# Opening of an attention stage on one Trainium2 core: constant rows by DMA, first columns loaded ahead on two queues, third heads' loads moved

## The chip, the cores and the metric

The program runs on one core of a Trainium2 chip, as one launch. The metric is the device time of one execution in microseconds (us). Beside each time stands a profile of one execution, taken by the hardware profiler.

## The reference, cut to what matters

The input x is 4 sequences of 2048 positions by 256 channels. The program computes one attention block and one mixture-of-experts block, each with a layer norm ahead and a residual around it:

```python
q_lat, k_lat, v_lat = x @ Wq_down, x @ Wk_down, x @ Wv_down   # 16 heads x 64
q = concat([q_lat @ Wq_up_c, rope(q_lat @ Wq_up_e)])          # 16 numbers a head
k = concat([k_lat @ Wk_up_c, rope(k_lat @ Wk_up_e)])
scores = (q @ k.T) / sqrt(16)                                 # causal, 2048 x 2048
y = softmax(scores) @ (v_lat @ Wv_up)
x = x + y @ Wc                                                # attention
x = x + sum over the top 2 of 8 experts (relu MLP, 256-512-256)
```

The change touches only the attention between the projections and y.

## The kernel before, in words

The program has several stages, one block each, with a barrier between them. `project` computes q, k and v for all heads and writes them to HBM (`parts_dram`, `v_dram`). `attend` reads them back and writes y. `mix` and the expert stage follow. In the profiled execution `project` ends and `attend` begins at about 284.8 us.

Fp32 accuracy comes from splitting q and k each into a high and a low part (`fp32r`). A head's stack in SBUF, in `q_st` and `k_st`, has three groups of 16 rows (`DH` = 16, `STACK` = 48): high, high, low of q against high, low, high of k. Two heads lie side by side in the partitions, one in partitions 0 to 63 and one in 64 to 127 (`par` 0 and 1, `HALF_ROWS` = 64). Rows 48 and 49 of each half are two more rows (`PARTS` = 2): in `q_st` they hold minus the row maximum of the scores, in two parts, and in `k_st` the constant 1.0, so that one matmul over 50 rows (`ROWS`) gives the score minus its maximum. The matmuls that only look for the maximum use the 48 rows.

The 16 heads of 4 sequences are worked through in 16 groups of four heads of one sequence (`NG` = 16, number w; three buffers, `BUFS` = 3, so group w uses buffer w % 3). One group is loaded by 13 DMAs on SP's queue (`load`, L717 to L731): 12 of 256 KB, each 16 rows by 2 head pairs by 2048 columns into 16 partitions of `q_st` or `k_st`, so packets of 8 KB; and one of 544 KB into `v_sb`, all 128 partitions. In the order of issue `q_st` and `k_st` alternate, so each set of 16 partitions is written by two DMAs in a row. All 13 increment the semaphore `loaded[u]`.

For each group the kernel does two passes. The maximum pass ("max" pieces): for a tile of 128 queries (`qt`, 16 of them), a pair of heads and a block of 512 keys (`kc`), two matmuls at L939 write a PSUM bank of `ps_m`, and VectorE (DVE) takes its maximum at L831 (whole blocks) or L835 (blocks on the diagonal, with the causal mask added). The tiles are taken in two turns: early (`qt` 0 to 11, `EARLY` = 12) and late (12 to 15). A turn ends with "chain" (L850, the negated maximum), "turn_max" (a transpose on TensorE at L946, the two parts at L860 and L862) and `place_minus` on SP: `minus_rows` goes to `minus_dram` (L736), SP waits for it, and two DMAs bring it into `q_st` rows 48 and 49 (L742). Only then may the scores pass of those queries start: matmuls at L904, exponentials on ScalarE (ACT) at L810 or L806, the diagonal mask on GpSimd (POOL) at L788, sums over the keys at L922 ("sum"), then "turn_out" (L950, L869, L874) and the store of y (L757).

All engines follow one list, `PLAN`, written by `attention_plan` from modelled costs. The change leaves it as it is. `SLOTS` = 2 banks of `ps_m` let TensorE be two pieces ahead of DVE.

The opening of the stage, which the change touches:

- POOL makes the identity, clears `maxes`, makes `causal`, then fills rows 32 to 63 of `k_st` with 1.0 for all three buffers (L778).
- DVE clears `ps_o` (L820), then fills rows 96 to 127 of `k_st` with 1.0 (L822). Each fill increments `ones_made`.
- SP waits for `ones_made` = 2 (L745), then issues the loads of groups 0, 1 and 2, 39 DMAs in a row, and goes on to the plan.
- TensorE (PE) waits for the identity, for `ones_made` = 2 and for `ps_o` to be clear. At the first max piece of a group it waits for all 13 DMAs of the load (`loaded[w % 3]` = 13 * 16).
- ACT has no work before the first scores.

The queues: SP's DMAs go to one hardware queue (q1 in the profile) over the core's 16 DMA engines. ACT's DMAs go to another. Both use the same 16 engines.

Of the kernel before, what the change touches and what calls it, by code (L numbers as in the profile page):

```python
# [15 lines left out]
TB = 512  # L16
# [622 lines left out]
def attend(nc, parts_dram, v_dram, minus_dram, y_dram):  # L639
# [17 lines left out]
    with ExitStack() as ctx:  # L657
        def sb(name, shape, dt):
            return ctx.enter_context(nc.sbuf_tensor(name, shape, dt))

        def sem(name):
            return ctx.enter_context(nc.semaphore(name))
# [10 lines left out]
        junk = sb("junk", [P, SLOTS, 2, TB], F32)  # L673
        maxes = sb("maxes", [P, GH, QT, CH], F32)
        minus = sb("minus", [P, GH * EARLY], F32)
        minus_rows = sb("minus_rows", [GH * EARLY, PARTS, P], F32R)

        ps_s = [ctx.enter_context(nc.psum_tensor(f"ps_s{i}", [P, 2 - i, 512], F32)) for i in range(2)]
# [3 lines left out]
        ident_made = sem("ident_made2")  # L682
        causal_made = sem("causal_made")
        ones_made = sem("ones_made")
        maxes_clear = sem("maxes_clear")
        banks_clear = sem("banks_clear")
        loaded = [sem(f"loaded{u}") for u in range(BUFS)]
# [26 lines left out]
        def turn_number(w, late):  # L714
            return 2 * w + (1 if late else 0)

        @block.sync  # L717
        def _(sp):
            def load(g):
                b, hg, u = g // HG, g % HG, g % BUFS  # L720

                for i, (of_q, of_k) in enumerate(((0, 0), (0, 1), (1, 0))):
                    for par in range(2):
                        rows = slice(par * HALF_ROWS + i * DH, par * HALF_ROWS + (i + 1) * DH)
                        for to, t, of in ((q_st, 0, of_q), (k_st, 1, of_k)):
                            sp.dma_start(to[rows, u, :, :].bitcast(F32),
                                         parts_v[t, of, :, :, hg:hg + 1, :, par, b * T:(b + 1) * T].rearrange(
                                             "f j g pr n -> (f j) (g pr) n")).then_inc(loaded[u], 16)
                sp.dma_start(v_sb[:, u, :, :, :].rearrange("p k h d -> p (k h d)"),
                             v_dram[hg, :, b * QT:(b + 1) * QT, :, :].rearrange("p k h d -> p (k h d)")  # L730
                             ).then_inc(loaded[u], 16)  # L731

            def place_minus(w, late):
                lo, n = (EARLY, QT - EARLY) if late else (0, EARLY)

                sp.dma_start(minus_dram[late][:, :, :, :].rearrange("s h k n -> (h k) s n"),  # L736
                             minus_rows[0:GH * n, :, :].bitcast(F32)).then_inc(rows_out, 16)
                sp.wait_ge(rows_out, 16 * (turn_number(w, late) + 1))
                from_v = minus_dram[late].rearrange("s (pr par) k n -> s pr par (k n)", par=2)
                for par in range(2):  # L740
                    rows = slice(par * HALF_ROWS + STACK, par * HALF_ROWS + ROWS)
                    sp.dma_start(q_st[rows, w % BUFS, :, lo * P:(lo + n) * P].bitcast(F32),  # L742
                                 from_v[:, :, par, :]).then_inc(rows_in, 16)

            sp.wait_ge(ones_made, 2)  # L745
            for g in range(BUFS):
                load(g)
            for e, ring in plan_with_ring():
                if e[0] == "turn_max":
                    sp.wait_ge(piece_taken, ring + 1)  # L750
                    place_minus(e[1], e[2])
                elif e[0] == "turn_out":
                    w, c = e[1] // CH, e[1] % CH
                    sp.wait_ge(piece_taken, ring + 1)
                    to = y_dram[(w // HG) * T + c * TB:(w // HG) * T + (c + 1) * TB,
                                (w % HG) * (GH * DH):(w % HG + 1) * (GH * DH)]
                    sp.dma_start(to.rearrange("(j p) n -> p j n", p=P),  # L757
                                 y_sb[:, c % 2, :, :, :].rearrange("p j h d -> p j (h d)")
                                 ).then_inc(y_stored[c % 2], 16)
                elif e[0] == "sum" and (e[1] + 1) % NSTEP == 0 and (e[1] + 1) // NSTEP + BUFS - 1 < NG:  # L760

                    sp.wait_ge(summed, e[1] + 1)
                    load((e[1] + 1) // NSTEP + BUFS - 1)
            for i in range(2):
                sp.wait_ge(y_stored[i], 16 * (NG * CH // 2))

        @block.gpsimd
        def _(pool):
            make_identity(nc, pool, ident, ident_made)
            nc.gpsimd.memset(maxes[:, :, :, :], NEG).then_inc(maxes_clear, 1)  # L770

            nc.gpsimd.memset(causal[:, :], 0.0).then_inc(causal_made, 1)
            pool.wait_ge(causal_made, 1)
            nc.gpsimd.affine_select(out=causal[:, TB - P:TB], in_=causal[:, TB - P:TB], compare_op=ALU.is_ge,
                                    fill=NEG, base=0, pattern=[[-1, P]],
                                    channel_multiplier=1).then_inc(causal_made, 1)
            pool.wait_ge(causal_made, 2)
            nc.gpsimd.memset(k_st[32:64, :, :, :].bitcast(F32), 1.0).then_inc(ones_made, 1)  # L778
            for s, (_, c, kt) in enumerate(STEP_LIST):
                r = kt - c * TILES  # L780
                if r < 0:
                    continue
                for pair in range(2):

                    pool.wait_ge(exp_made, COVERS[s][2 * pair + 1] + 1)
                    at = (s % PROBS) * GH + 2 * pair
                    tile = prob[:, at:at + 2, r * P:(r + 1) * P]
                    nc.gpsimd.affine_select(out=tile, in_=tile, compare_op=ALU.is_ge, fill=0.0, base=0,  # L788
                                            pattern=[[0, 2], [1, P]], channel_multiplier=-1).then_inc(masked, 1)

        @block.scalar
        def _(act):
            for e in PLAN:
                if e[0] == "scores":
                    k = e[1]
                    bank = ps_s[k % 2]
                    newest = GROUPS[k][-1][0]
                    if newest >= PROBS:

                        act.wait_ge(summed, newest - PROBS + 1)  # L800
                    act.wait_ge(scores_made, k + 1)
                    at = (GROUPS[k][0][0] % PROBS) * GH + GROUPS[k][0][1]
                    lows = [STEP_LOW[s] for s, _ in GROUPS[k]]
                    if len(lows) == 2 and lows[0] != lows[1]:
                        for i, lo in enumerate(lows):
                            last_exp = nc.scalar.activation(prob[:, at + i, lo:TB], bank[:, i, lo:TB], ACT.Exp,  # L806
                                                            scale=DH ** -0.5)
                    else:
                        n, lo = len(lows), lows[0]
                        last_exp = nc.scalar.activation(prob[:, at:at + n, lo:TB], bank[:, 0:n, lo:TB], ACT.Exp,  # L810
                                                        scale=DH ** -0.5)
                    last_exp.then_inc(exp_made, 1)
                elif e[0] == "sum" and STEP_LAST[e[1]]:

                    act.wait_ge(summed, e[1] + 1)
                    nc.scalar.copy(out_sb[:, STEP_LIST[e[1]][1], :], ps_o[:, :]).then_inc(out_copied, 1)

        @block.vector
        def _(dve):
            nc.vector.memset(ps_o[:, :], 0.0).then_inc(banks_clear, 1)  # L820

            nc.vector.memset(k_st[96:128, :, :, :].bitcast(F32), 1.0).then_inc(ones_made, 1)  # L822
            dve.wait_ge(causal_made, 2)
            dve.wait_ge(maxes_clear, 1)

# [52 lines left out]
        @block.tensor  # L878
        def _(pe):
            pe.wait_ge(ident_made, 2)  # L880
            pe.wait_ge(ones_made, 2)
            pe.wait_ge(banks_clear, 1)

            def half(par, rows):
                return slice(par * HALF_ROWS, par * HALF_ROWS + rows)

            loads_seen = rows_seen = 0
            for e, ring in plan_with_ring():
                slot = ring % SLOTS
                if e[0] == "scores":  # L890
                    k = e[1]
                    w, c, _ = STEP_LIST[GROUPS[k][-1][0]]
                    placed = turn_number(w, c == CH - 1) + 1
                    if placed > rows_seen:

# [13 lines left out]
                elif e[0] == "sum":  # L909
                    s = e[1]  # L910
                    w, c, kt = STEP_LIST[s]
                    r = kt - c * TILES
                    lo = STEP_LOW[s]
                    if STEP_FIRST[s] and s:

                        pe.wait_ge(out_copied, CH * w + c)
# [9 lines left out]
                else:  # L926
# [3 lines left out]
                        pe.wait_ge(piece_taken, ring - SLOTS + 1)  # L930
                    if e[0] == "max":
                        _, w, qt, pair, kc = e
                        if w + 1 > loads_seen:

                            pe.wait_ge(loaded[w % BUFS], LOADS * 16 * (w // BUFS + 1))
                            loads_seen = w + 1
# [988 lines left out]
```

## Time and profile before

| | us |
|---|---|
| three timed runs | 2747.91, 2764.52 (median), 2771.68 |
| the profiled execution | 2749.61 |
| its span, first to last instruction | 2747.7 |
| start of `attend` in it | 284.8 |
| first load DMA issued | 298.43 |
| first max matmul | 329.43 |
| first scores matmul | 391.41 |
| PE, DVE, ACT, POOL busy (us of the span) | 2398.2, 2107.0, 1569.7, 772.5 |

The profiled execution took 1.9 us more than its span. Times in the rows below are microseconds from the start of the span. PE is TensorE's matmul, PEld its weight load, DVE is VectorE, ACT is ScalarE, POOL is GpSimd. SPq, ACTq and POOLq are the DMA-issuing instructions of those engines.

### The profile page before, as it was taken

To read this page: it belongs to the slowest core of one execution; us is meant where nothing else is said; L and a number is where in the kernel's file an instruction comes from. 1 tells how busy PE (TensorE), PEld (TensorE's weight loads), DVE (VectorE), ACT (ScalarE), POOL (GpSimd) and SP (SyncE) were. 2 spreads that over 40 slices of the span, in tenths; PEclk is the share of its full clock that TensorE was granted. 3 is DMA by queue.
4 is the path that set the end of the run, shared out by engine and by line. 5 is a ranking of instruction groups with operands and counts; after the bars stand their busy time and mean duration, and the time that the engine had idled before them with its cause. 6 is when DMAs were issued, how large, how long until landed. Compare 5 with 4: busy or idle time off the path is not lost. (4 is left out here: it accounts for less than half of the span.)

```text
span 2747.7 us, 49305 instructions
## 1 busy us (share of the span) xinstructions
PE 2398.2 (87%) x15842; PEld 1364.3 (50%) x15842; DVE 2107.0 (77%) x5154; ACT 1569.7 (57%) x2668; POOL 772.5 (28%) x1051
## 2 busy tenths in 40 slices
PE   6777179999999999999999999999879669999997
PEld 6666033333333333333333333333246458889896
DVE  3998398999899888887888998896038657777775
ACT  2444016777677677676667777777745424444442
POOL 1555200110110110110110110110107646766553
PEclk7888559999899999998899999999989879999999
DMA  4999760431430440440431440400059633333332
GB/s 149 338 335 319 126 83 5 63 46 23 61 50 19 61 60 9 61 59 10 61 40 29 63 51 17 64 7 6 9 226 263 170 114 105 105 118 107 113 110 64
DMA packets 154501, 255.60 MB, mean 93 GB/s; under 512 B 72563, under 2 KB 95605, under 8 KB 145568
## 3 DMA queue, kind: packets, MB, share of 16 engines
q1 hardware_dynamic: 129760, 191.47, 32.3%
q0 software_dynamic: 22736, 55.48, 6.1%
q10 hardware_dynamic: 1776, 5.72, 0.5%
q8 instruction: 129, 2.11, 0.4%
q14 instruction: 100, 0.82, 0.1%
HBM read 147.59 MB, written 107.76 MB: 93 GB/s over the span
## 5 line engine op out<-in xcount | busy, mean ns | idle before, releaser
L810 ACT ACTIVATE prob<-ps_s 128x512 f32<-128x512 f32 (+5 forms) x1620 | 1078.4, 714 | 522.2 <-PE ps_s L904 519.3
L831 DVE TENSOR_REDUCE maxes<-ps_m 128x2 f32<-128x1024 f32 x768 | 913.7, 1221 | 117.1 <-PE ps_m L939 114.2
L939 PE MATMUL ps_m<-k_st,q_st 48*128 48x512 f32 (+3 forms) x2560 | 611.8, 447 | 115.4 <-DMA v_sb<-v_dram 58.4
L904 PE MATMUL ps_s<-q_st,k_st 50*128 50x512 f32 (+3 forms) x2560 | 612.4, 414 | 74.6 <-ACT prob L810 56.8
L788 POOL TENSOR_SCALAR_AFFINE_SELECT prob<-prob 128x256 f32<-128x256 f32 x512 | 203.2, 406 | 1485.9 <-ACT prob L810 1355.2
L922 PE MATMUL ps_o<-prob,v_sb 128*17 128x512 f32 (+3 forms) x5120 | 618.6, 557 | 1.2 <-ACT prob L810 0.7
L939 PEld LDWEIGHTS ps_m<-k_st,q_st 48*128 48x128 f32 x2560 | 278.1, 194 | 577.3 <-DVE maxes L831 257.1
L835 DVE CUSTOM_DVE_ANT_0 junk<-ps_m,causal 128x128 f32<-128x128 f32 (+3 forms) x1024 | 453.2, 484 | 76.0 <-PE ps_m L939 74.0
L904 PEld LDWEIGHTS ps_s<-q_st,k_st 50*128 50x128 f32 x2560 | 320.5, 191 | 300.7 <-ACT prob L810 228.8
L1703 ACT ACTIVATE h_hi<-ps_turned 128x512 fp32r<-128x512 f32 x142 | 85.0, 598 | 214.2 <-PE ps_turned L1820 214.2
L922 PEld LDWEIGHTS ps_o<-prob,v_sb 128*17 128x17 f32 x5120 | 86.9, 96 | 171.6 <-issue 143.0
L91 PE MATMUL ps_out<-experts_hi,h_lo 128*128 (+1 forms) x568 | 171.7, 302 | 0.0
L93 PE MATMUL ps_out<-experts_hi,h_hi 128*128 (+1 forms) x568 | 160.4, 282 | 0.0
L92 PE MATMUL ps_out<-experts_lo,h_hi 128*128 (+1 forms) x568 | 160.0, 282 | 0.0
L1735 DVE TENSOR_TENSOR h<-ps_hidden,b_sb 128x512 f32<-128x512 f32 x142 | 98.2, 691 | 45.5 <-PE ps_hidden L93 44.7
L1749 DVE TENSOR_TENSOR y<-ps_out,b_sb 128x256 f32<-128x256 f32 x142 | 60.3, 424 | 87.7 <-PE ps_out L93 87.2
L91 PE MATMUL ps_hidden<-experts_hi,x_lo 128*128 (+1 forms) x284 | 126.0, 444 | 0.7 <-issue 0.5
L1124 POOL DMA_INDIRECT list_dram<-entry,slots x100 | 96.8, 968 | 79.2 <-DVE slots L1388 52.1
L93 PE MATMUL ps_hidden<-experts_hi,x_hi 128*128 (+1 forms) x284 | 113.0, 398 | 0.0
L92 PE MATMUL ps_hidden<-experts_lo,x_hi 128*128 (+1 forms) x284 | 112.9, 398 | 0.0
L92 PEld LDWEIGHTS ps_out<-experts_lo,h_hi 128*128 128x128 f32 x568 | 107.6, 189 | 0.1
L869 DVE RECIPROCAL rec<-ps_m 128x16 f32<-128x16 f32 x64 | 16.2, 253 | 118.9 <-PE ps_m L950 118.0
(183 smaller groups left out, 3181.4 us busy)
## 6 DMA issues: line engine op xcount, KB each, us to landing
parts_dram<-parts SPq DMA_DIRECT2D x64, 512.0 KB, 3.6
q_st<-parts_dram SPq DMA_DIRECT2D x96, 256.0 KB, 15.4
k_st<-parts_dram SPq DMA_DIRECT2D x96, 256.0 KB, 17.1
v_dram<-v_out SPq DMA_DIRECT2D x16, 544.0 KB, 4.7
v_sb<-v_dram SPq DMA_DIRECT2D x16, 544.0 KB, 25.4
xin<-in_L_attn_x SPq DMA_DIRECT2D x16, 512.0 KB, 4.7
ffn_raw<-in_L_ffn_W SPq DMA_DIRECT2D x32, 256.0 KB, 4.9
split_hi<-ffn_hi SPq DMA_DIRECT2D x16, 512.0 KB, 4.9
```

The source lines that it names most:

```text
L91: nc.tensor.matmul(out, s_lo, m_hi, start=first, stop=False, skip_group_check=True)
L92: nc.tensor.matmul(out, s_hi, m_lo, start=False, stop=False, skip_group_check=True)
L93: return nc.tensor.matmul(out, s_hi, m_hi, start=False, stop=last, skip_group_check=True)
L788: nc.gpsimd.affine_select(out=tile, in_=tile, compare_op=ALU.is_ge, fill=0.0, base=0, pattern=[[0, 2], [1, P]], channel_multiplier=-1).the ...
L810: last_exp = nc.scalar.activation(prob[:, at:at + n, lo:TB], bank[:, 0:n, lo:TB], ACT.Exp, scale=DH ** -0.5)
L831: return nc.vector.tensor_reduce(maxes[:, 2 * pair:2 * pair + 2, qt, kc], bank[:, :, :], AX.X, ALU.max)
L835: last = nc.vector.tensor_tensor_reduce(junk[:, slot, i, 0:w], bank[:, i, 0:w], causal[:, TB - w:TB], 1.0, NEG, ALU.add, ALU.max, maxes[:, ...
L904: mm = nc.tensor.matmul(ps_s[k % 2][:, i, lo:TB], k_st[half(h % 2, ROWS), w % BUFS, h // 2, kt * P:(kt + 1) * P], q_st[half(h % 2, ROWS), ...
L922: mm = nc.tensor.matmul(ps_o[32 * h:32 * h + VW, lo:TB], v_sb[:, w % BUFS, kt, h, :], prob[:, (s % PROBS) * GH + h, lo:TB], start=STEP_FIR ...
L939: mm = nc.tensor.matmul(ps_m[slot][:, i, 0:wide], q_st[half(i, STACK), w % BUFS, pair, qt * P:(qt + 1) * P], k_st[half(i, STACK), w % BUFS ...
L1124: pool.indirect_dma_start(list_dram[:, :], bass.IndirectOffsetOnAxis(ap=slots[:, j, i:i + 1], axis=0), entry[:, j, i, :], None).then_inc(s ...
L1735: nc.vector.tensor_tensor(out=h[:, s % 2, :], in0=ps_h[s % 2][:, :], in1=b1_sb[:, bass.ds(e, 1), :].rearrange("p a n -> p (a n)"), op=ALU. ...
```

## The change

What it does:

- A new tile `ones` (2 partitions by 2048) is filled with 1.0 by DVE, in place of the two fills of 32 partitions by 12288. ACT brings it into rows 48, 49 and 112, 113 of `k_st` by two DMAs of 96 KB each, all three buffers at once (`ones_placed`).
- The loads of group 0 are cut by columns. Columns 0 to 511 come first: six DMAs of 64 KB for `q_st` on SP's queue and six for `k_st` on ACT's queue, all on `first_loaded`. The remaining 1536 columns (twelve DMAs of 192 KB) and v (544 KB) follow on SP's queue.
- Group 1 is loaded by ACT's queue, after the constant rows. Group 2 is loaded by SP's queue, issued after the `place_minus` of the first turn. In all loads the six DMAs of `q_st` now come before the six of `k_st`, and consecutive DMAs write different sets of 16 partitions.
- SP waits for nothing at its start. PE waits for `first_loaded` before the plan, for `loaded[0]` at the first max piece with `qt` of 4 or more, and for `ones_placed` before the first scores. The wait for `loaded` is also looked at by the "sum" entries.

```diff
+        ones = sb("ones", [PARTS, T], F32)
...
+        def load_heads(eng, g, t, lo, hi, done):
+            b, hg, u = g // HG, g % HG, g % BUFS
+            to, pieces = ((q_st, (0, 0, 1)), (k_st, (0, 1, 0)))[t]
+
+            for i, of in enumerate(pieces):
+                for par in range(2):
+                    rows = slice(par * HALF_ROWS + i * DH, par * HALF_ROWS + (i + 1) * DH)
+                    eng.dma_start(to[rows, u, :, lo:hi].bitcast(F32),
+                                  parts_v[t, of, :, :, hg:hg + 1, :, par, b * T + lo:b * T + hi].rearrange(
+                                      "f j g pr n -> (f j) (g pr) n")).then_inc(done, 16)
+
+        def load(eng, g):
+            b, hg, u = g // HG, g % HG, g % BUFS
+            for t in range(2):
+                load_heads(eng, g, t, TB if g == 0 else 0, T, loaded[u])
+            eng.dma_start(v_sb[:, u, :, :, :].rearrange("p k h d -> p (k h d)"),
+                          v_dram[hg, :, b * QT:(b + 1) * QT, :, :].rearrange("p k h d -> p (k h d)")
+                          ).then_inc(loaded[u], 16)
+
         @block.sync
...
-            sp.wait_ge(ones_made, 2)
-            for g in range(BUFS):
-                load(g)
+            load_heads(sp, 0, 0, 0, TB, first_loaded)
+            load(sp, 0)
             for e, ring in plan_with_ring():
                 if e[0] == "turn_max":
                     sp.wait_ge(piece_taken, ring + 1)
                     place_minus(e[1], e[2])
+                    if turn_number(e[1], e[2]) == 0:
+                        for g in range(2, BUFS):
+                            load(sp, g)
...
-            nc.gpsimd.memset(k_st[32:64, :, :, :].bitcast(F32), 1.0).then_inc(ones_made, 1)
...
         @block.scalar
         def _(act):
+            load_heads(act, 0, 1, 0, TB, first_loaded)
+            act.wait_ge(ones_made, 1)
+            for par in range(2):
+                rows = slice(par * HALF_ROWS + STACK, par * HALF_ROWS + ROWS)
+                act.dma_start(k_st[rows, :, :, :].bitcast(F32).rearrange("p u a n -> p (u a) n"),
+                              ones[:, :].unsqueeze(1).broadcast_to([PARTS, BUFS * 2, T])).then_inc(ones_placed, 16)
+            load(act, 1)
...
-            nc.vector.memset(k_st[96:128, :, :, :].bitcast(F32), 1.0).then_inc(ones_made, 1)
+            nc.vector.memset(ones[:, :], 1.0).then_inc(ones_made, 1)
...
-            pe.wait_ge(ones_made, 2)
             pe.wait_ge(banks_clear, 1)
...
+            pe.wait_ge(first_loaded, LOADS // 2 * 2 * 16)
             for e, ring in plan_with_ring():
...
+                    if k == 0:
+                        pe.wait_ge(ones_placed, 2 * 16)
...
+                    if w + 1 > loads_seen:
+                        pe.wait_ge(loaded[w % BUFS], LOADS * 16 * (w // BUFS + 1))
+                        loads_seen = w + 1
...
-                        if w + 1 > loads_seen:
+                        if w + 1 > loads_seen and (w or qt >= TILES):
```

## Rows read from the trace of the kernel before

**Rows 1.** The page, parts 1 and 2: busy time, and the DMA engines' share in 40 slices.
```profile
PE 2398.2 (87%) x15842; PEld 1364.3 (50%) x15842; DVE 2107.0 (77%) x5154; ACT 1569.7 (57%) x2668; POOL 772.5 (28%) x1051
...
DMA  4999760431430440440431440400059633333332
```

**Rows 2.** Waits of all engines, 284 to 330: engine line waited for, total, times, longest.
```profile
PE ps_m L939 <- DMA v_sb<-v_dram: 58.4, 1, 58.4
```

**Rows 3.** Waits of SP's own queue, 280 to 384.
```profile
SPq L726 <- DVE k_st L822: 13.7, 1, 13.7
```

**Rows 4.** Timeline, 276 to 394: start, duration, engine line operation.
```profile
284.81 0.20 POOL L98 MEMSET ident<- 128x128 f32 x1 [6.78 <-POOLq L121]
...
288.10 10.30 DVE L822 MEMSET k_st<- 32x12288 f32 x1 [2.62 <-issue]
298.43 0.37 SPq L726 DMA_DIRECT2D q_st<-parts_dram  x1
298.84 0.42 SPq L726 DMA_DIRECT2D k_st<-parts_dram  x1
299.31 0.42 SPq L726 DMA_DIRECT2D q_st<-parts_dram  x1
...
303.50 0.42 SPq L726 DMA_DIRECT2D k_st<-parts_dram  x1
303.96 0.42 SPq L729 DMA_DIRECT2D v_sb<-v_dram  x1
...
311.90 1.07 SPq L726 DMA_DIRECT2D k_st<-parts_dram  x1
```

**Rows 5.** DMA issues of four short windows from 298.2 on: us from issue to landing.
```profile
q_st<-parts_dram SPq DMA_DIRECT2D x1, 256.0 KB, 4.6
k_st<-parts_dram SPq DMA_DIRECT2D x1, 256.0 KB, 6.3
q_st<-parts_dram SPq DMA_DIRECT2D x1, 256.0 KB, 8.2
...
v_sb<-v_dram SPq DMA_DIRECT2D x1, 544.0 KB, 25.3
k_st<-parts_dram SPq DMA_DIRECT2D x1, 256.0 KB, 23.9
```

**Rows 6.** Windows: PE, PEld, DVE, ACT, POOL busy, granted clock, DMA share, GB/s.
```profile
6.00:9.00 3.00, 0.00 (x0) 0.00 (x0) 0.00 (x0) 0.00 (x0) 0.00 (x0) 1.00 1.04 430
...
300.30:327.40 27.10, 0.00 (x0) 0.00 (x0) 0.00 (x0) 0.00 (x0) 0.00 (x0) 0.50 1.02 123
```

**Rows 7.** DMA issues of 0 to 20: SP's queue beside POOL's.
```profile
down<-in_L_attn_Wk_down SPq DMA_DIRECT2D x1, 1024.0 KB, 8.9
down<-in_L_attn_Wv_down SPq DMA_DIRECT2D x1, 1024.0 KB, 13.9
...
cos<-in_rope_cos POOLq DMA_DIRECT2D x1, 1024.0 KB, 9.1
```

**Rows 8.** Timeline of DVE, 329 to 425.
```profile
330.09 0.29 DVE L835 CUSTOM_DVE_ANT_0 junk<-ps_m,causal 128x128 f32<-128x128 f32 x1 [31.69 <-PE ps_m L939]
...
337.23 1.22 DVE L831 TENSOR_REDUCE maxes<-ps_m 128x2 f32<-128x1024 f32 x1
...
381.22 0.35 DVE L850 TENSOR_REDUCE minus<-maxes 128x48 f32<-128x192 f32 x1
...
421.10 0.28 DVE L835 CUSTOM_DVE_ANT_0 junk<-ps_m,causal 128x128 f32<-128x128 f32 x1
```

**Rows 9.** Timeline, 384 to 407: SP's queue and the first scores.
```profile
384.37 0.31 SPq L736 DMA_DIRECT2D minus_dram<-minus_rows  x1
385.97 1.51 SPq L742 DMA_DIRECT2D q_st<-minus_dram  x2
391.41 1.05 PE L904 MATMUL ps_s<-q_st,k_st 50*128 50x512 f32 x3
406.11 0.40 SPq L757 DMA_DIRECT2D y_dram<-y_sb  x1
```

More of the change, by code:

```diff
@@ L684, in attend @@
         ones_made = sem("ones_made")
+        ones_placed = sem("ones_placed")
+        first_loaded = sem("first_loaded")
         maxes_clear = sem("maxes_clear")
@@ L715, in turn_number @@
             return 2 * w + (1 if late else 0)
+        def load_heads(eng, g, t, lo, hi, done):
[14 more added lines that the diff above has]
+                          ).then_inc(loaded[u], 16)
         @block.sync
         def _(sp):
[L719 to L731, printed above, removed]
             def place_minus(w, late):
@@ L762, in _ @@
                     sp.wait_ge(summed, e[1] + 1)
-                    load((e[1] + 1) // NSTEP + BUFS - 1)
+                    load(sp, (e[1] + 1) // NSTEP + BUFS - 1)
             for i in range(2):
```

## The prediction

> **What bounds the kernel now.** I read the page first: PE is the busiest engine over the whole span, 87%, DVE is at 77%, and the DMA engines are full only in the first slices, around one tenth of the span and at the start of the last stage [rows 1]. A share over the span says nothing of the opening of one stage, so next come the waits in the stretch where `attend` begins. One wait is far longer than all others: PE sits idle 58.4 us before its first max matmul, until the load of v of group 0 has landed [rows 2]. The stage itself begins at 284.8, when POOL comes through the barrier [rows 4]. The queue's own waits say why the load came so late: SP waited 13.7 us for DVE's fill of `k_st`, which runs from 288.1 to 298.4 [rows 3, 4]. So the opening has three parts: 13.7 us of fill, from 284.8 to 298.4; 31 us of load, from 298.4 to 329.4; and then the maximum pass of the first turn, which DVE bounds: its pieces follow each other from 330.1 to the chain at 381.2 [rows 8]. The scores start at 391.4 after the trip of the maxima through HBM [rows 9]. Nothing of the later work can start before that, so what the opening gains or loses goes into the time in full.
>
> **The load in numbers.** The first 256 KB were issued at 298.43 and landed 4.6 us later, at 303.0; the twelfth was issued at 303.50 and landed 23.9 later, at 327.4; v landed at 303.96 + 25.3 = 329.3 [rows 4, 5]. Eleven DMAs in 24.4 us are 2.22 us for each 256 KB, 118 GB/s, and v took 1.9 us. The first one's 4.6 us less 2.2 leave 2.4 us from issue until data flow. In this stretch the 16 DMA engines show as fully busy (1.02) at 123 GB/s, while in the first microseconds of the program they moved 430 at the same share [rows 6]. The engines are thus full with transfers that write 16 partitions each, and slow ones.
>
> **Change, part 1: the start without the fill.** The fills of 10.3 us on POOL and DVE go. SP and ACT issue their first DMAs at about 284.8. Data flow from 287.2. The first columns are 12 x 64 KB = 768 KB, three units of 256 KB: 3 x 2.22 = 6.7 us, so 293.9. DVE's first piece follows 0.8 us after landing, as at 329.3 to 330.1 [rows 5, 8], at 294.7. The eight pieces of the first four tiles took from 330.09 to 337.23, 7.1 us [rows 8], so they end at 301.8, where DVE was at 337.2 before. If the rest of group 0 were there, 35.4 us would be gained. It is not: what is late next is the load of the other 1536 columns.
>
> **Part 2: the rest of group 0 beside group 1.** This decides. SP's queue holds 12 x 192 KB = 2304 KB and v; ACT's queue holds 12 x 256 KB = 3072 KB and v. ACT can issue them from about 290 on: DVE's fill starts at 288.1 and a fill of 2048 columns in place of 12288 takes a sixth of 10.3, 1.7 us. So both queues flow from about 294, with as many packets (6 KB against 8 KB). How do two queues share the engines? In the first stage SP's queue and POOL's ran side by side. Wv_down, issued one step of 0.5 us behind Wk_down, took 13.9 us to land against 8.9: 5.5 us for its 1.05 MB, while `cos` was on its way by POOL's queue [rows 7] and the engines moved 430 GB/s, 2.4 MB in 5.5 us [rows 6]. SP's queue had a little under half, and the engines' share stood at 1.04 [rows 6]. With equal shares of packets, the rest of group 0 ends only when group 1 is nearly in: 5376 KB, 21 units of 256 KB, 21 x 2.22 = 46.6 us, and 2 x 1.9 = 3.8 for both v. That is 344.3, and DVE takes its first whole block 1.0 us later, at 345.3. Before it was at 337.2: **8.1 us later than before**, at the old rate. In general, with r the rate of both queues together over the old 118 GB/s, DVE resumes at 293.9 + 3.8 + 1.0 + 46.6 / r and the change is 46.6 / r - 38.5 us. It is nothing at r = 1.21.
>
> **What r is.** The trace of before has no two queues with 16-partition writes, so it is bounded. Low: the k_st DMA that follows a q_st DMA on the same partitions lands 2.1 us after it (303.0 to 305.1), the one that turns to new partitions 2.4 us later (305.1 to 307.5) [rows 4, 5]. Now every DMA turns to new ones; at 2.4 us each, r = 2.22 / 2.4 = 0.925, and the change is +11.9 us. High: v, over all 128 partitions, went at 544 KB in 1.9 us, 2.5 times the rate [rows 5], so the engines can do more when more partitions are written at once. If the queues did not disturb each other at all, SP's needs 9 x 2.22 = 20.0 us and v 1.9: group 0 is in at 315.8, DVE resumes at 316.8, 20.4 us earlier. I take r = 1.1, nearest to the row in which two queues gave no more than one, with a little for engines that write different partitions at one moment: 42.4 - 38.5 = **+3.9 us**.
>
> The Trainium skill has a rule that speaks against this change. "SBUF — State Buffer", section "Can I just issue two DMAs to hit both halves?", says that two concurrent DMAs to partitions 0 and 64 gave only 6% more than one, since both run on the same 16 engines. By that, r is 1.06 and the sum 44.0 - 38.5 = +5.5 us, an estimate from that page. No row here shows it for these writes.
>
> **Part 3: constant rows.** Two DMAs of 96 KB into two partitions. The nearest row is the pair that brings the maxima into two partitions: 2 x 24 KB, issued from 385.97, and the scores start at 391.4, so at most 5.4 us for 48 KB [rows 9]. Four times the bytes are at most 22 us; at the rate of the 16-partition DMAs they would be 1.7 us. Issued at 290 they are in by 312, and needed at about 391. Cost nothing, with 80 us of cover. What they do to the queue behind them is a rival below.
>
> **Part 4: order, ACT's issues, group 2.** ACT issues 6 + 2 + 13 DMAs of some 0.47 us [rows 4], 10 us in all, while it has no other work until 391. SP's issues began to take longer (1.07) only at the 29th in a row [rows 4]; ACT has 21 and SP 19. Group 1 is in by 344 to 366 and wanted at 421.1 [rows 8]. Group 2's 13 DMAs are issued after SP's row DMAs at about 387.5, for 6.1 us, and SP's next work is the store at 406.1 [rows 9]. Its bytes then flow for some 28 us beside the scores, where before they were over at 385.6. Behind them in the queue stands the store of y, which may land some 10 us late; nothing waits for it until that buffer is used again two stores on. At nothing, up to 1 us if a row DMA meets them. The extra waits on PE are met when it comes there. From DVE's resumption on, the 43.9 us to the chain at 381.2 and all after it stay as they are.
>
> **Sum.** Start earlier, load shared: +3.9 us. The profiled execution, 2749.6, would be 2753.5. It is at the lower end of what was shown; the median of the runs is 14.9 above it. The mean of all four executions is 2758.4, and with +3.9 that gives 2762, which I forecast. It lies between the sums made on the profiled execution and on the median (2768).
>
> **Rivals.** (a) The queues add up, or nearly: r of 1.5 to 2 or more, -7.4 to -20.4 us. For it: v's rate, and that each set of 16 partitions is a bottleneck of its own. Against: rows 7, and engines that are busy at 1.02 with one queue. 2738 in full. (b) Slower: the turn to new partitions costs at each DMA, in the load of group 0; r under 1, price +11.9 us at 0.925; it decides from r below 1.21 on. For it: 2.4 against 2.1. Against: those two may be one lag seen twice. 2770. (c) Group 1 trails. If the two constant DMAs hold ACT's queue for 10 us, SP's queue moves 4.5 units alone; 10.5 are left, 23.3 / 1.1 = 21.2 us; group 0 is in at 293.9 + 10 + 21.2 + 3.8 = 328.9, DVE resumes at 329.9: -7.3 us, 2751. For it: writes into two partitions are slow. Against: nothing shows that they hold all 16 engines. That the start does not come forward at all is excluded by the wait for the fill, which is the only one between the barrier and the first load.
>
> **How the numbers follow.** Forecast (r 1.0 to 1.3, -3 to +8 us) 0.45, (a) 0.25, (b) 0.15, (c) 0.15. The forecast's own range is 2756 to 2767. The range runs from (a), 2758.4 - 20.4 = 2738, to (b) on the mean of the four, 2770, and 6 more because a median of a few runs may lie that far above the mean, as it does here: 2776. One per cent is 27 us, about what a measurement of this kernel can tell from no change; even (a) is only 20 us. Faster by over 1%: 0.04; within 1%: 0.93; slower: 0.03.
>
> **What would show it.** SP's first issue at 285. A first DVE piece at 293 to 296; if later, part 1 is wrong. Then a second wait of PE on a DMA, from about 302 to X, where X is group 0's landing: 340 by the forecast, 316 by (a), 348 by (b), 329 by (c). GB/s between 294 and 340: near 130 by the forecast, above 200 by (a). The first scores at 391.4 + 3.9 = 395.3. Wrong would be a wait anywhere after the scores start that grew by more than 2 us.

## The result, and the profile after

The changed kernel takes 2741.52 us (median of 20 runs, 2715.57 to 2771.07), the kernel before 2757.69 (20 runs, 2734.73 to 2782.83): ratio 0.9927, 95% interval 0.9901 to 0.9953. The ratio leaves out runs more than 1.5% above the fastest of their kernel (slow ones), so it gives 20 us, where the medians of all runs differ by 16. I forecast 2762 and a change of +3.9 us. The number lies in my range, the direction is wrong.

The profiled execution took 2743.78 us, its span 2741.9. The opening does almost what the prediction said. First the waits of all engines in 276 to 400:

```profile
PE ps_m L960 <- DMA v_sb<-v_dram: 39.5, 1, 39.5
PE ps_m L960 <- DMA k_st<-parts_dram: 22.3, 1, 22.3
```

Where before one wait of 58.4 us stood [rows 2], there are two, 62 us together. The timeline of the same stretch:

```profile
285.64 2.79 ACTq L727 DMA_DIRECT2D k_st<-parts_dram  x6
285.65 0.20 POOL L98 MEMSET ident<- 128x128 f32 x1 [6.78 <-POOLq L121]
...
288.52 1.96 ACTq L806 DMA_DIRECT2D k_st<-ones  x2
...
294.21 0.69 PE L960 MATMUL ps_m<-k_st,q_st 48*128 48x128 f32 x4 [22.32 <-DMA k_st<-parts_dram]
...
339.97 0.90 PE L960 MATMUL ps_m<-k_st,q_st 48*128 48x512 f32 x4 [39.50 <-DMA v_sb<-v_dram]
...
395.00 1.05 PE L922 MATMUL ps_s<-q_st,k_st 50*128 50x512 f32 x3
```

The first columns are in at 294.1 (forecast 293.9, for a stage that starts 0.8 us earlier), the rest of group 0 at 339.9 (forecast 340), the first scores start at 395.0 (forecast 395.3; before 391.4 [rows 9]). So the opening is 3.6 us later on the clock of the span, 2.7 us longer from the stage's start. It is not where the gain is. The window of 300 to 340:

```profile
300.00:340.00 40.00, 0.50 (x4) 0.06 (x2) 2.09 (x8) 0.00 (x0) 0.00 (x0) 0.50 0.96 140
```

Two queues move 140 GB/s, against 123 with one [rows 6]. Both windows hold some of v's bytes, which flow faster. In windows that end before v begins to flow (at 324.8), before and after, it is 117 against 136:

```profile
301.00:324.00 23.00, 0.00 (x0) 0.00 (x0) 0.00 (x0) 0.00 (x0) 0.00 (x0) 0.50 1.02 117
```

```profile
296.00:324.00 28.00, 3.41 (x12) 1.30 (x10) 5.94 (x24) 0.00 (x0) 0.00 (x0) 0.50 1.02 136
```

The gain lies behind the opening. `minus_dram<-minus_rows` (L736, now L744) happens twice for each group of heads, so it marks the time like a clock. Lines of it from SP's timeline, of before:

```profile
483.05 0.32 SPq L736 DMA_DIRECT2D minus_dram<-minus_rows  x1
...
578.04 0.32 SPq L736 DMA_DIRECT2D minus_dram<-minus_rows  x1
...
1906.62 0.33 SPq L736 DMA_DIRECT2D minus_dram<-minus_rows  x1
```

and of after:

```profile
387.95 0.31 SPq L744 DMA_DIRECT2D minus_dram<-minus_rows  x1
...
486.75 0.32 SPq L744 DMA_DIRECT2D minus_dram<-minus_rows  x1
...
581.64 0.32 SPq L744 DMA_DIRECT2D minus_dram<-minus_rows  x1
...
1893.78 0.33 SPq L744 DMA_DIRECT2D minus_dram<-minus_rows  x1
```

From the first to the last it is 384.37 to 1906.62 = 1522.3 us before [rows 9] and 1505.8 after: 16.5 us less in a part of the program in which the change leaves the work of PE, DVE, ACT and POOL alone; only the order of DMAs within a load and the place of group 2's load differ. From there to the end of the span the profiled execution of the changed kernel is 7.0 us longer (848.1 against 841.1), so the two profiled executions differ by 5.8 us in all, and their mean granted clocks are 0.924 before and 0.923 after: one pair of traces does not show the whole gain. In an undisturbed group there is no difference (578.04 - 483.05 = 95.0 us before; 581.64 - 486.75 = 94.9 after). The differences, of both signs, are in the groups in which the granted clock falls in one kernel and not in the other; most of the 16.5 us comes between 1111 and 1480. One such place is the load of a group near 1206. SP's timeline of before:

```profile
1212.14 0.42 SPq L729 DMA_DIRECT2D v_sb<-v_dram  x1
1212.61 0.43 SPq L736 DMA_DIRECT2D minus_dram<-minus_rows  x1
1236.94 1.23 SPq L742 DMA_DIRECT2D q_st<-minus_dram  x2
1238.21 2.95 SPq L757 DMA_DIRECT2D y_dram<-y_sb  x3
```

A turn's rows are written right behind the thirteen DMAs of a load, in the same queue. They land when the load has landed, 24 us later. SP waits for them, and three stores of y stand behind that wait. Then the windows of before, with PE, PEld, DVE, ACT, POOL busy, granted clock, DMA share and GB/s:

```profile
1236.00:1240.00 4.00, 3.46 (x28) 1.63 (x24) 2.93 (x7) 2.80 (x7) 1.22 (x3) 1.00 0.22 50
1240.00:1244.00 4.00, 3.17 (x20) 1.47 (x20) 3.20 (x7) 1.40 (x5) 1.17 (x3) 0.70 0.23 53
1244.00:1248.00 4.00, 4.00 (x26) 1.80 (x26) 1.98 (x5) 1.83 (x4) 0.77 (x2) 0.50 0.00 0
1248.00:1252.00 4.00, 3.46 (x18) 1.91 (x18) 3.03 (x7) 2.97 (x4) 0.00 (x0) 0.50 0.00 0
1252.00:1256.00 4.00, 4.00 (x21) 0.97 (x13) 2.31 (x6) 1.35 (x3) 0.00 (x0) 0.59 0.01 4
```

and of after:

```profile
1236.00:1240.00 4.00, 3.92 (x32) 1.63 (x24) 3.38 (x8) 2.80 (x6) 1.22 (x3) 1.00 0.22 52
1240.00:1244.00 4.00, 3.19 (x32) 1.73 (x33) 3.50 (x10) 2.17 (x7) 1.82 (x5) 1.00 0.24 55
1244.00:1248.00 4.00, 3.42 (x27) 1.57 (x23) 3.73 (x11) 3.51 (x5) 0.11 (x1) 1.00 0.00 0
1248.00:1252.00 4.00, 4.00 (x30) 1.42 (x28) 3.55 (x7) 2.79 (x5) 0.00 (x0) 1.00 0.01 4
```

PE's first matmul behind the wait, before and after:

```profile
1240.83 0.50 PE L939 MATMUL ps_m<-k_st,q_st 48*128 48x512 f32 x2 [1.37 <-DVE y_sb L874]
```

```profile
1240.81 0.50 PE L960 MATMUL ps_m<-k_st,q_st 48*128 48x512 f32 x2 [0.89 <-DVE y_sb L890]
```

Before, PE idled for 1.4 us until DVE had written `y_sb`, which waited 1.1 us for a store of y; then the clock was granted at 0.50, the lower of its two levels (1.2 GHz), for some 14 us. In 1244 to 1248 PE looks full (4.00), while DVE is busy for 1.98 us where it is 3.73 after. After, the same wait is there, but shorter (0.6 us of DVE, 0.9 of PE), and no fall follows. Over 395 to 1960 the waits of DVE for a store of y, before and after:

```profile
DVE y_sb L874 <- DMA y_dram<-y_sb: 4.9, 5, 1.6
```

```profile
DVE y_sb L890 <- DMA y_dram<-y_sb: 0.8, 2, 0.6
```

So the theory that the experiments had to test was: the new order of the DMAs in a load makes each later load some 2 to 3 us shorter (31.0 us before and 28.6 after, from first issue to landing, as the mean of the thirteen later loads), fewer stores of y come too late, and the granted clock falls less often.

### The profile page after: what moved, and what is told of

Read it like the earlier page. It is cut to its first block and busy times, and to the rows that moved or that the text cites. A ratio compares the mean times of both kernels' runs of the same rounds, so it can differ in the third digit from the quotient of the medians.

```text
span 2741.9 us, 49320 instructions
## 1 busy us (share of the span) xinstructions
PE 2395.7 (87%) x15842; PEld 1360.0 (50%) x15842; DVE 2098.7 (77%) x5154; ACT 1570.1 (57%) x2668; POOL 762.0 (28%) x1050
```

## The experiments

All were timed beside the kernel before. They ran on three chips, on which the kernel before itself takes 2871 to 2882 us (medians of 27 to 29 runs), so only their ratios are compared with the result and with each other.

**The changed kernel again.** 

> The changed kernel once more. Its first profile shows the first scores at 395.0 (before: 391.4), so an opening that is 3 us longer, but the timed runs are 0.73% (20 us) faster. Theory A (the profiled execution is not typical, the landing of group 0 varies from execution to execution): here the landing is 15 us or more away from 339.9. Theory B (the new order of DMAs in the loads of all later groups helps) and theory C (the granted clock in the rest of the attention is higher): landing within 3 us of 339.9 again, ratio near 0.993. If the 0.73% was chance, ratio within 0.3% of 1.

Ratio 0.9928 (0.9892 to 0.9963). PE resumed at 341.4 and the scores began at 396.4, 112.1 us after the stage start (109.4 in the first profile, 106.6 before). The gain is real and the late landing is typical: theory A falls. In this profile DVE waited 1.6 us for a store at 1239, and the lower clock followed for 14 us: the changed kernel is not free of these falls.

**The order alone.** The kernel before with

```diff
-                for i, (of_q, of_k) in enumerate(((0, 0), (0, 1), (1, 0))):
-                    for par in range(2):
-                        rows = ...
-                        for to, t, of in ((q_st, 0, of_q), (k_st, 1, of_k)):
+                for to, t, ofs in ((q_st, 0, (0, 0, 1)), (k_st, 1, (0, 1, 0))):
+                    for i, of in enumerate(ofs):
+                        for par in range(2):
+                            rows = ...
```

> The kernel before with the new order of DMAs in every load and nothing else. Theory B: ratio 0.992 to 0.995, with fewer or shorter falls of the granted clock after the first scores. Theories A and C: within 0.3% of 1; the opening then shows what the order alone does to the rate: first max matmul at 329.4 if the order is worth nothing, 2 to 3 us later if each turn to new partitions costs 2.4 us in place of 2.2, earlier by 2 us or more if alternating partitions is a gain.

Ratio 0.9941 (0.9902 to 0.998): nearly the whole gain of the change, with nothing of its new opening. The wait for group 0 and a window in the load:

```profile
PE ps_m L939 <- DMA v_sb<-v_dram: 55.6, 1, 55.6
```

```profile
298.00:321.00 23.00, 0.00 (x0) 0.00 (x0) 0.00 (x0) 0.00 (x0) 0.00 (x0) 0.50 1.02 135
```

PE waits 2.8 us less than the 58.4 of before [rows 2], and the load runs at 135 GB/s where the like window of before has 117, on one queue. The expected sign of fewer or shorter falls is not in this kernel's one profile, which is among its slower runs: the mean granted clock over 395 to 1960 is 0.96, as before. Over all its runs the mean clock is higher (0.9148 against 0.9101).

**Only the fill taken away.** Constant rows by two small DMAs on ACT's queue, SP's 39 loads at once, in the old order.

```diff
-            sp.wait_ge(ones_made, 2)
...
+            act.wait_ge(ones_made, 1)
+            for par in range(2):
+                rows = slice(par * HALF_ROWS + STACK, par * HALF_ROWS + ROWS)
+                act.dma_start(k_st[rows, :, :, :]..., ones[:, :]...).then_inc(ones_placed, 16)
```

> The kernel before with constant rows by two small DMAs on ACT's queue; SP starts its 39 loads at once in the old order, on one queue, nothing cut by columns. All theories agree on the opening: first max matmul at 329.4 - 13.7 = 315.7, first scores at 377.7. If the opening passes into the time in full the ratio is 0.995 (-13.7 us). Less than half of that would say that the opening's gain is given back later, by the granted clock or by waits.

Ratio 0.9992 (0.9955 to 1.003), and the opening did not move. SP's first issue and PE's first matmul:

```profile
285.17 0.37 SPq L728 DMA_DIRECT2D q_st<-parts_dram  x1
```

```profile
330.98 0.69 PE L945 MATMUL ps_m<-k_st,q_st 48*128 48x128 f32 x4 [59.57 <-DMA v_sb<-v_dram]
```

Group 0 took 45.8 us in place of 31. The 208 increments of its semaphore show why: 199 are there at 316.0, 15 us before the last, and the last eight come in four pairs from 318.7 to 330.8, as if two of the sixteen engines were far behind the others. All theories had missed this. In the changed kernel only the last pair lags, by 4 us (335.7 to 339.8).

**The constant rows issued after group 0.** The same, with ACT waiting for group 0 first:

```diff
             act.wait_ge(ones_made, 1)
+            act.wait_ge(loaded[0], LOADS * 16)
```

> The fill-only experiment with the two constant DMAs issued after group 0 has landed. There two of the 16 engines' shares of group 0 landed 15 us late. If the constant rows cost this, group 0 lands 31 us after the stage start (at 316), the opening is 13.7 us shorter than before and the ratio is 0.995. If they did not, it lands at 331 again and the ratio is near 1.

```profile
315.34 0.69 PE L946 MATMUL ps_m<-k_st,q_st 48*128 48x128 f32 x4 [45.06 <-DMA v_sb<-v_dram]
...
381.63 1.19 PE L911 MATMUL ps_s<-q_st,k_st 50*128 50x512 f32 x3 [4.11 <-DMA q_st<-minus_dram]
```

Group 0 is in 31.3 us after the stage start at 284.0, so the two small DMAs had cost 14.5 us of transfer time. The first scores then wait 4.1 us for their rows, which stand behind the load of group 2 in SP's queue, so the opening is 9.0 us shorter than before (97.6 against 106.6), not 13.7. The ratio is 0.9891 (0.9853 to 0.993), but its ten runs have a median of 2883, no lower than that of the kernel before (2882), and spread from 2841 to 2898, so whether the shorter opening shows in the time stays open.

**Group 1 waits for group 0.** The changed kernel with

```diff
+            act.wait_ge(loaded[0], LOADS * 16)
             load(act, 1)
```

> The changed kernel, but ACT waits until group 0 has landed before it loads group 1. If the two queues share one rate, as I forecast, group 0 lands at 294 + 20.0 + 1.9 = 316 in place of 340, and the first scores come at 371, 24 us earlier than in the changed kernel. Theory A or C with an opening that passes in full: 24 us under the changed kernel, ratio to before about 0.984. If two queues had added up, group 0 would land where it does now, and nothing would change.

```profile
316.91 0.90 PE L961 MATMUL ps_m<-k_st,q_st 48*128 48x512 f32 x4 [16.65 <-DMA v_sb<-v_dram]
```

Group 0 landed 23 us earlier than in the changed kernel, so the two queues do share one rate, and the first scores begin at 371.9 (expected 371). The rate of one queue alone is seen best in the kernel with all three edits (below), where neither group 1 nor the constant rows are on their way:

```profile
294.00:307.00 13.00, 3.89 (x12) 1.64 (x12) 6.22 (x28) 0.00 (x0) 0.00 (x0) 0.50 1.04 129
```

In such windows one queue moves 129, 131 and 135 GB/s in the three kernels with the new order, and two queues 126 to 137 in four. One queue in the old order moves 116 to 122 in five. Ratio 0.9839 (0.9772 to 0.9906), from six runs.

**Rows ahead of a load.** The kernel before, old order; SP keeps the load of a later group back until the next turn's rows are placed:

```diff
                     place_minus(e[1], e[2])
+                    if held is not None:
+                        sp.wait_ge(summed, held + 1)
+                        load((held + 1) // NSTEP + BUFS - 1)
+                        held = None
```

> The kernel before, old order of DMAs, old opening; only SP issues the load of a later group after the next turn's rows (place_minus) in place of ahead of them. Theory B1 (rows of a turn that stand behind a load in SP's queue land late, PE starves some 30 us after the load's start, and the granted clock falls after it; the new order helps since it ends the load 3 us earlier): as fast as the order alone or faster, ratio 0.990 to 0.995. Theory B2 (it is the length of the load or its rate that matters, not what stands behind it): within 0.3% of 1.

Ratio 0.993 (0.9896 to 0.9964), as much as the order gave. SP's own waits for the rows' first leg, of before and of this kernel:

```profile
SPq L742 <- DMA minus_dram<-minus_rows: 140.7, 31, 24.7
```

```profile
SPq L742 <- DMA minus_dram<-minus_rows: 40.1, 31, 2.8
```

One wait of 4.6 us for a store of y is left in it, where a load is issued just ahead of three stores.

**The same partitions for longer.** Four DMAs in a row write the same 16 partitions or those 32 further on, for two before.

```diff
+                for turns in (((0, 0, 0), (2, 1, 0)), ((1, 0, 1),)):
+                    for par in range(2):
+                        for to, t, i, of in ...:   # q and k of i = 0, then of i = 2; then i = 1
```

> The kernel before with an order of DMAs that stays on the same partitions, or on those 32 further on, for four DMAs in a row where the old order stays for two. If the rate follows how often the target partitions change, the load of group 0 takes 0.5 to 2 us longer than before (31 us) and the whole is slower by 0 to 0.5%. If the rate does not depend on it, the first max matmul stays at 329.4 after a stage start at 284.8 and the ratio at 1.

The wait for group 0 is 60.0 us, 1.6 longer. Ratio 1.0004 (0.9958 to 1.0049), with a median of 2895.5 against 2881.9: at most a little slower, and not told apart from before. Its waits for stores of y are the longest of all, and in one place (the same load, here at 1220) the chain is seen whole, in the waits over 395 to 1960, PE's timeline and the windows:

```profile
DVE y_sb L875 <- DMA y_dram<-y_sb: 14.3, 8, 3.2
```

```profile
1255.49 0.79 PE L940 MATMUL ps_m<-k_st,q_st 48*128 48x512 f32 x2 [3.41 <-DVE y_sb L875]
```

```profile
1252.00:1255.00 3.00, 0.08 (x2) 0.00 (x0) 0.00 (x0) 1.01 (x3) 0.77 (x2) 0.93 0.39 89
1255.00:1260.00 5.00, 4.51 (x28) 2.06 (x28) 3.68 (x10) 1.32 (x4) 0.90 (x3) 0.50 0.13 28
1260.00:1265.00 5.00, 4.46 (x30) 2.31 (x22) 3.15 (x7) 2.66 (x4) 0.27 (x1) 0.50 0.00 0
1265.00:1270.00 5.00, 5.00 (x20) 2.07 (x20) 3.13 (x7) 1.89 (x4) 0.00 (x0) 0.50 0.01 3
```

PE idles for 3.4 us, the clock is at its lower level for more than 15.

**Four buffers for y.** The kernel before with `y_sb` and `y_stored` four deep, so that DVE finds a free buffer when a store is late.

```diff
-        y_sb = sb("y_sb", [P, 2, TILES, GH, DH], F32)
+        y_sb = sb("y_sb", [P, YBUFS, TILES, GH, DH], F32)
```

> The kernel before with four buffers for y in place of two, so that DVE no longer waits for a store of y that stands behind a load and behind the wait for a turn's rows in SP's queue. In the trace of before DVE waited 5 times for it, 4.9 us in all, with the old order in two more kernels 8.5 and 9.0, with the new order 0.8 to 2.3, with the same-partitions order 14.3. If this wait is the seed of the falls of the granted clock during the loads: no such wait, ratio 0.990 to 0.995 like the order alone and rows first. If it is not: within 0.3% of 1.

Ratio 0.9939 (0.9905 to 0.9973). The rows still land late, SP still waits 143.5 us for them, the loads are as long as before; only the wait of DVE is gone from the trace, and with it as much time as the order saved. The interval leaves the size wide, 8 to 27 us, and the waits alone are 5 to 9 us in four traces with the old order, so the part of the gain that comes from what follows a wait could be small.

Falls without such a wait are there too. The two longest of before, and the longest of the kernel with four buffers for y, in which DVE never waits for a store:

```profile
700.00:720.00 20.00, 19.88 (x101) 8.41 (x101) 12.88 (x32) 9.98 (x19) 3.59 (x9) 0.57 1.00 115
1322.00:1342.00 20.00, 18.98 (x100) 8.09 (x98) 13.37 (x33) 9.68 (x18) 3.18 (x8) 0.57 1.01 114
```

```profile
534.00:575.00 41.00, 40.42 (x175) 16.01 (x174) 25.05 (x56) 20.30 (x28) 1.81 (x5) 0.50 0.01 4
```

**The old order put back for the later groups.** The changed kernel, groups 3 to 15 in the old order (the diff is the loop of the kernel before for `g >= BUFS`).

> The changed kernel, but groups 3 to 15 are loaded in the old order. The opening should be as in the changed kernel, first scores some 109 us after the stage start (before: 106.6). If the whole gain of the change comes from the order of the later loads, nothing is left of it: ratio 0.998 to 1.003. If the opening carries it in any way, 0.993.

Ratio 0.999 (0.9952 to 1.0028), and DVE waits for stores again, 6.6 us in five places. The first scores begin at 397.0, 112.1 us after the stage start. The median of its twelve runs is 2880 against 2871. Nothing of the gain is left that this interval can show: it came from the order of the loads of groups 3 to 15. The opening is 5.5 us longer here than before, and no gain of its own is in it.

**Group 2 early.** The changed kernel with group 2 issued behind group 0.

```diff
             load(sp, 0)
+            for g in range(2, BUFS):
+                load(sp, g)
```

> The changed kernel with group 2 issued by SP right behind group 0. Its bytes flow from 340 to 368, over before the first turn's rows at 388, so moving it is worth nothing in this opening: ratio within 0.3% of the changed kernel's 0.993. If it were needed, the first scores would come later by a wait for the rows, as the 4.1 us in the fill-rows-late experiment, whose opening was 15 us shorter.

Ratio 0.9915 (0.9881 to 0.9948), as in the changed kernel. The first scores meet no wait for their rows. Group 0 landed at 343.9 here, its last pair of increments 10 us behind the rest, and the scores began 113.9 us after the stage start, 2 to 5 us later than in the two profiles of the changed kernel. The time shows no difference either way.

**Together.** The changed kernel with constant rows and group 1 after group 0 and rows ahead of the later loads; then the same with four buffers for y.

> The changed kernel with constant rows and group 1 issued after group 0 has landed, and later groups loaded after a turn's rows. Group 0 should land at 312 to 313 (316.9 with group 1 waiting alone, less 4.5 us by which two engines lagged), first scores near 367. By theory B1 the rest of the attention is as in the changed kernel or better: ratio to before 0.978 to 0.984.

> All-three (constant rows and group 1 after group 0, loads after a turn's rows) with four buffers for y. The one wait of 2.7 us for a store that was left goes; the fall of the clock behind it should go too. Ratio to before 0.975 to 0.982.

PE resumes at 311.6 in the first, the scores begin at 366.7. The ratios are 0.9804 (0.9764 to 0.9844) and 0.9845 (0.9802 to 0.9888), from six runs each and measured against different sets of runs of before; the two are not told apart, and the first not from the kernel in which only group 1 waits (0.9839). Both intervals end below that of the changed kernel's ratio, which begins at 0.9901: either version beats both kernels.

## Why the prediction was wrong

**Part 1, the start without the fill: right.** Landing, first piece and resumption came within 1 us of the working.

**Part 2, r: right in size, wrong in its reason, and lucky.** From 46.6 / r with r = 1.1 I had the landing at 340 and it was at 339.9. But I gave the 10% to two queues that write different partitions at a time. In windows without v one queue moved 116 to 122 GB/s in the old order and 129 to 135 in the new one, and two queues in the new order 126 to 137: the order gave the gain, and the second queue nothing that these runs can show. And all but two of the 208 increments were in at 335.7; the last 4 us are the lag beside the constant rows, which I had put at nothing. The rule of the Trainium skill that I had set beside the sum ("SBUF — State Buffer", "Can I just issue two DMAs to hit both halves?": two DMAs serialize) agrees with these traces: 126 to 137 GB/s with two queues against 129 to 135 with one. Whether two give the page's 6% more is not told by runs that differ by as much among themselves.

**Rival (b) had the sign of the row wrong.** I read 2.4 us against 2.1 between landings as the price of turning to new partitions. With more turns the load was faster, by 2.8 us in 31, and with fewer slower, by 1.6.

**Part 3, the constant rows "cost nothing": wrong, and hidden.** Beside a lone queue in the old order they cost 14.5 us. With group 1 waiting, moving them behind group 0 too brought group 0 in 27.5 us after the stage start in place of 31.1. In the changed kernel the last increments lag 4 us, which the fit of r covered. Rival (c), that they would favour group 0, has it the wrong way round.

**The step that failed** is the last sentence of part 4: "From DVE's resumption on, the 43.9 us to the chain at 381.2 and all after it stay as they are." The diff changes the order of the DMAs in all thirteen later loads, and I had read it as a matter of the opening, as the title says, and put everything behind the opening at nothing. Had I carried the order through, I would have found a load in SP's queue ahead of a turn's rows, SP blocked at the rows and stores of y behind it. In the trace of before the five waits of DVE for a store, 4.9 us in all, would still have looked too small to matter. The lower clock follows three of them, for about 3, 7 and 14 us, and not the other two (at 626 and 1553). That makes 24 us of the 126 that the clock is at its lower level in 395 to 1960; since that level is half of the other, at most 12 us of time. In place of "stay as they are" the later loads gave the whole change: about -20 us by the measured ratio (-16 by the medians), with the opening's own +3 in it, which I had forecast as +3.9.

What is shown: undoing the order in the later loads takes the whole gain away; the order alone gives it; and three different cures of one chain (a shorter load, rows ahead of the load, buffers for y) each give 0.6 to 0.7%. Nor do they clearly add up: rows ahead and the constant rows moved, on top of the new order and a waiting group 1, gave 0.9804 against 0.9839, with intervals that overlap. The size of each is uncertain by more than half, though: the order alone lies between 6 and 28 us. How the chain turns into this much time is not shown. The clock's falls are read from traces and not isolated: a fall could not be forbidden with the waits left in. Falls without such a wait are there in every kernel, and they vary from one execution to the next.

## What to carry to other kernels

Follow an edit in a helper through every call of it, not only through the place that the change is about. Ask of each small DMA what is queued ahead of it, and of each wait of a queue-issuing engine what stands behind it: here a load of 31 us held up rows, the rows held up SP, SP the stores, the stores DVE, and all that showed was five waits of 1 us. Read the granted clock in windows over the whole span: a short starvation can have a fall of the clock behind it that costs more than the wait, and falls that have nothing to do with the change can hide or feign a difference of less than 1% in a pair of traces.

## What the runs showed of the hardware that I had not expected

Within a kernel the time of a run follows its mean granted clock closely. Over the 71 runs of the first four experiments and of the kernel before beside them, a fit with one level for each kernel gives 2.2 us more for each 0.001 less of mean clock, with 4.6 us left over as scatter. The kernel before had 0.9101 on average there, the changed kernel 0.9172 and the order alone 0.9148. By that slope the clock would go with 15 of the changed kernel's 20 us and 10 of the order's 21 (between mean times). It does not tell kernels apart by itself: the kernel with only the fill taken away had 0.9140 and was no faster than before.

The order in which 16-partition DMAs take their partitions sets the rate of one queue: 116 to 122 GB/s with two in a row on the same 16 partitions, 129 to 135 with none.

Two DMAs of 96 KB into two partitions held back two engines' shares of a transfer by 15 us, although all the other engines had finished theirs; a load is in when its slowest engine is.
